# Two ConvLSTM recurrences: eighteen matmuls over 112 rows against fourteen over 128 packed rows per cell

## The reference, cut to what matters

```python
def step(carry, xr):
    h, c = carry
    inp = jnp.concatenate([xr, h], axis=1)          # 96 channels
    gates = lax.conv_general_dilated(inp, w_mid, (1,), 'SAME', dimension_numbers=dn) + b[None, :, None]
    i, f, g, o = jnp.split(gates, 4, axis=1)         # 4 x 48 channels, 3 taps along the width
    c2 = jax.nn.sigmoid(f) * c + jax.nn.sigmoid(i) * jnp.tanh(g)
    h2 = jax.nn.sigmoid(o) * jnp.tanh(c2)
    return ((h2, c2), h2)
_, hs = lax.scan(step, (z, z), x_rows, reverse=reverse)
```

## Time and profile before

| what | value |
|---|---|
| median of three runs | 2088.05 us (2082.49 to 2180.3) |
| the profiled execution's own time | 2081.32 us |
| its span, first to last instruction | 2079.5 us |
| around the span | 1.8 us |
| mean granted TensorE clock | 0.943 of full speed |
| first and last matmul of L668 | 278.1 and 1488.0 us |
| busy: TensorE, VectorE, ScalarE, GpSimd | 1838.4, 1388.5, 1064.7, 708.4 us |

### The profile page before, as it was taken

One profiled execution on the slowest core, in us unless ns is written; L12 is line 12 of the kernel. 1 busy time (PEld: TensorE's weight loads), 2 busy tenths in 40 slices (PEclk: granted clock), 3 DMA queues, 4 the chain that ended last, 5 costly groups with the idle time before them and its releaser, 6 DMA issues. The chain is left out here.

```text
span 2079.5 us, 43778 instructions
## 1 busy us (share of the span) xinstructions
PE 1838.4 (88%) x16306; PEld 1197.7 (58%) x16306; DVE 1388.5 (67%) x2550; ACT 1064.7 (51%) x1961; POOL 708.4 (34%) x583
## 2 busy tenths in 40 slices
PE   6979269999999999509999999999835999999999
PEld 5545147777777777207777777777512545555555
DVE  5538968888888888457888888888674234333434
ACT  1116147777777776346777777777561222222320
POOL 2010046666666655225666666665300000000000
PEclk9999679999999999759999999999976999999999
DMA  1769320000000000850000000000193001110100
GB/s 65 258 197 213 98 61 23 23 23 23 23 23 23 24 23 10 136 145 25 23 23 23 23 23 23 24 23 23 21 183 82 18 18 33 33 28 23 33 18 26
DMA packets 74618, 111.10 MB, mean 53 GB/s; under 512 B 11856, under 2 KB 31152, under 8 KB 74512
## 3 DMA queue, kind: packets, MB, share of 16 engines
q1 hardware_dynamic: 74512, 109.50, 20.3%
HBM read 71.71 MB, written 37.75 MB: 53 GB/s over the span
## 5 line engine op out<-in xcount | busy, mean ns | idle before, releaser
L668 PE MATMUL gates_l<-xh_l,w_hi_l 112*112 112x512 f32 x3072 | 819.5, 402 | 117.1 <-DVE keep_l L730 117.1
L668 PEld LDWEIGHTS gates_l<-xh_l,w_hi_l 112*112 112x112 f32 x3072 | 537.7, 175 | 315.4 <-issue 117.8
L644 POOL TENSOR_TENSOR xh_l<-xf_l,xh_l 48x512 fp32r<-48x512 f32 x256 | 360.1, 1407 | 281.8 <-ACT xh_l L687 281.4
L668 PE MATMUL gates_l<-xh_l,w_lo_l 112*112 112x512 f32 x1536 | 450.5, 402 | 0.0
L639 POOL TENSOR_TENSOR xh_l<-hs,xh_l 48x512 fp32r<-48x512 f32 x254 | 303.2, 1194 | 173.8 <-DVE hs L759 173.8
L668 PEld LDWEIGHTS gates_l<-xh_l,w_lo_l 112*112 112x112 f32 x1536 | 270.1, 176 | 97.9
L1174 PE MATMUL b_dw<-b_hid,b_diag 32*32 32x512 f32 x9120 | 313.1, 599 | 0.0
L699 ACT ACTIVATE gate_if_l<-gates_l 112x512 f32<-112x512 f32 x256 | 153.0, 598 | 246.9 <-PE gates_l L668 246.9
L739 DVE TENSOR_TENSOR keep_l<-gate_if_l,cell_l 48x512 f32<-48x512 f32 x256 | 175.5, 685 | 140.8 <-ACT gate_if_l L699 140.8
L1174 PEld LDWEIGHTS b_dw<-b_hid,b_diag 32*32 32x32 f32 x9120 | 185.7, 103 | 116.0 <-issue 48.3
L748 DVE TENSOR_TENSOR cell_l<-keep_l,add_l 48x256 f32<-48x256 f32 x512 | 196.7, 428 | 26.6
(11 more groups left out here) (148 smaller groups left out, 1236.4 us busy)
## 6 DMA issues: line engine op xcount, KB each, us to landing
xf_l<-rows SPq DMA_DIRECT2D x256, 96.0 KB, 2.0
hs<-rows SPq DMA_DIRECT2D x32, 384.0 KB, 10.3
rows<-hs SPq DMA_DIRECT2D x32, 384.0 KB, 5.0
xr<-in_x_rows SPq DMA_DIRECT2D x24, 256.0 KB, 2.7
xc<-in_x_cols SPq DMA_DIRECT2D x24, 256.0 KB, 3.0
mixed<-stage SPq DMA_DIRECT2D x24, 256.0 KB, 3.0
edged<-stage SPq DMA_DIRECT2D x24, 256.0 KB, 3.2
mixed_sb<-mixed SPq DMA_DIRECT2D x32, 192.0 KB, 3.7
```

The lines of the kernel that those rows point to most:

```text
L644: pool.tensor_tensor(xh[far[d]:far[d] + C, d, s, 1, :, 1:W + 1], xf[far[d]:far[d] + C, s, :].rearrange("p (b w) -> p b w", b=B), xh[far[d] ...
L668: mm = nc.tensor.matmul(ps[d][m][0:K, :], weight[:, d, m, t, :], xh[0:K, d, s, part, :, t:t + W], start=(first and t == 0), stop=(last and ...
```

## The change

- **The products are packed into 128 partitions.** The unused 16 + 16 rows of the operand (partitions 48 to 63 and 112 to 127) get channels 0 to 31 of the rounded x row, and the remaining 16 channels get a tile `xc` of their own, in which the three taps stand below each other (3 x 16 rows, twice, and two rows of ones for the bias). A cell step then has seven operands for each of the two banks: q = 0 on `xc`; q = 1 to 3, one for each tap, on a tile "HI" = [hi of h | lo of x | hi of x, channels 0 to 31]; q = 4 to 6 on a tile "LO" = [lo of h | hi of h again | the same x rows]. 2 x 7 = 14 matmuls. The weights lie in one tile `w` of 128 x 3136, staged through the unused part of `hs`; a `mask` says for which rows of q = 0 to 3 the rounded weight is subtracted from the whole one (which gives lo) and for which not.
- **DMAs bring the packed rows.** `spread(d, s)` on SyncE: four DMAs from one SBUF tile to another for each cell step, after TensorE is done with the tiles of that row. The x rows of both directions are loaded into one tile.
- **VectorE computes the state once, unrounded, in two halves into `hs` (L841). ScalarE rounds it from there into the HI tile, in two halves (L749, `state_hi`), and copies it once more into the LO tile (L756, `copy_state`)**, both while it works on the other direction's step: rounding between the sigmoid of i, f and the tanh of g, copy between that tanh and the sigmoid of o.
- **The rounding of the x rows goes to VectorE** (L819), one instruction for both directions, once per row instead of two.
- The tanh of g stays in PSUM and is multiplied there (L773, L830), and `cell` is one bank, added in one instruction (L834).

The diff, cut to its core:

```diff
--- before.py
+++ after.py
+        raw = hs[:, H // 2:H // 2 + WROWS, :].rearrange("p a n -> p (a n)")[:, 0:NW]
+        w = sb("w", [P, 2, NCH, 2, K], F32R)
...
-        xh = sb("xh", [P, 2, 2, 2, B, WP], F32R)
+        xs = sb("xs", [P, 2, FLAT + 2 * LEAD], F32R)
+        xh = sb("xh", [P, 2, 2, 2, FLAT], F32R)
+        xc = sb("xc", [P, 2, 2, FLAT], F32R)
...
+                def spread(d, s):
+
+                    for a in range(2):
+                        some = x_rows(s, slice(far[d] + a * GAP, far[d] + (a + 1) * GAP)).bitcast(F32)
+                        sp.dma_start(xh[a * HALF + C:(a + 1) * HALF, d, s, :, :].bitcast(F32), some.unsqueeze(1).broadcast_to([GAP, 2, FLAT])
+                                     ).then_inc(x_spread[d][s], 16)
+                    rest = xs[far[d] + 2 * GAP:far[d] + C, s, LEAD - 1:LEAD - 1 + FLAT].bitcast(F32)
+                    shifts = bass.AP(rest.tensor, rest.offset, [list(rest.ap[0]), [1, 3], [1, FLAT]])
+                    for c in range(2):
+                        sp.dma_start(xc[3 * GAP * c:3 * GAP * (c + 1), d, s, :].bitcast(F32), shifts).then_inc(x_spread[d][s], 16)
...
+                        if s < more:
+
+                            sp.wait_ge(x_lo[0], ahead)
+                            sp.wait_ge(x_lo[1], ahead)
+                            load(row_f, row_b, 1 - s)
+                        for d in range(2):
+                            sp.wait_ge(gates[d][1], done)
+                            if d == 0:
+                                sp.wait_ge(x_hi, split)
+                            spread(d, s)
...
+                    pool.wait_ge(x_hi, t + 1)
+                    if not (isinstance(t, int) and t < 2):
+                        pool.wait_ge(gates[d][1], t - 1)
+                    pool.tensor_tensor(inner(xh[f:f + C, d, s, HI, :]), wide(xf[f:f + C, s, :]),
+                                       inner(x_rows(s, slice(f, f + C))).bitcast(F32), ALU.subtract).then_inc(x_lo[d], 1)
...
+                            pe.wait_ge(x_spread[d][s], SPREAD * k + SPREAD)
+                            pe.wait_ge(sig_if[d], 2 * k + (s + 1))
+                            pe.wait_ge(sig_o[d], 2 * k + (s + 1))
+                            pe.wait_ge(cells[d], 2 * k + (s + 1))
+                            for m in range(2):
+                                chunk(m, 0, xc[:, d, s, :], 1, first=True)
+                            pe.wait_ge(x_lo[d], 2 * k + (s + 1))
+                            pe.wait_ge(h_hi[d], 2 * k + (s + 1))
+                            for m in range(2):
                                 for t in range(3):
-                                    mm = nc.tensor.matmul(ps[d][m][0:K, :], weight[:, d, m, t, :],
-                                                          xh[0:K, d, s, part, :, t:t + W],
-                                                          start=(first and t == 0), stop=(last and t == 2))
-                                return mm
+                                    chunk(m, 1 + t, xh[:, d, s, HI, :], t)
+                            pe.wait_ge(h_copy[d], 2 * k + (s + 1))
+                            pe.wait_ge(h_lo[d], 2 * k + (s + 1))
                             for m in range(2):
-                                taps(m, w_hi, 0, True, False)
-                                taps(m, w_lo, 0, False, False)
-                            pe.wait_ge(h_lo[d], 2 * k + s + 1)
-                            for m in range(2):
-                                taps(m, w_hi, 1, False, True).then_inc(gates[d][m], 1)
+                                for t in range(3):
+                                    mm = chunk(m, 4 + t, xh[:, d, s, LO, :], t, last=(t == 2))
+                                mm.then_inc(gates[d][m], 1)
...
+                def state_hi(t, row, d, s):
+
+                    n = near[d]
+                    for j, part in enumerate(parts):
+                        act.wait_ge(h_full[d], t * 2 + (j + 1))
+                        hi = nc.scalar.activation(padded(xh[n:n + C, d, s, HI, :])[:, j * HB:(j + 1) * HB, 1:W + 1],
+                                                  state(row, d)[:, part].rearrange("p (b w) -> p b w", b=HB), ACT.Copy)
+                    hi.then_inc(h_hi[d], 1)
+
+                def copy_state(row, d, s):
+
+                    f = far[d]
+                    nc.scalar.activation(inner(xh[f:f + C, d, s, LO, :]), wide(state(row, d)), ACT.Copy).then_inc(h_copy[d], 1)
...
+                            act.wait_ge(gates[d][0], 2 * k + (s + 1))
                             nc.scalar.activation(gate_if[0:K, d, :], ps[d][0][0:K, :], ACT.Sigmoid).then_inc(sig_if[d], 1)
...
+                            if some:
+                                state_hi(earlier, row, 1 - d, slot)
+                            act.wait_ge(gates[d][1], 2 * k + (s + 1))
+                            nc.scalar.activation(ps[d][1][n:n + C, :], ps[d][1][n:n + C, :], ACT.Tanh).then_inc(tanh_g[d], 1)
+                            if some:
+                                copy_state(row, 1 - d, slot)
+                            nc.scalar.activation(gate_o[f:f + C, d, :], ps[d][1][f:f + C, :], ACT.Sigmoid).then_inc(sig_o[d], 1)
+                            act.wait_ge(cells[d], 2 * k + (s + 2))
                             for j, part in enumerate(parts):
-                                act.wait_ge(cells[d], 4 * k + 2 * s + (j + 3))
...
+                                nc.scalar.activation(tanh_c[f:f + C, j, 0:PART], cell[f:f + C, part],
                                                      ACT.Tanh).then_inc(tanhs[d], 1)
...
+                    nc.vector.tensor_copy(w[:, d].rearrange("p a b c -> p (a b c)"), raw[:, d * per_d:(d + 1) * per_d]
+                                          ).then_inc(w_hi, 1)
...
+                    dve.wait_ge(w_hi, d + 1)
+                    for q, chunks in enumerate((slice(0, 1), slice(1, 4))):
+                        part = w[:, d, chunks].rearrange("p a b c -> p (a b c)")
+                        whole = raw[:, d * per_d + chunks.start * 2 * K:d * per_d + chunks.stop * 2 * K]
+                        nc.vector.scalar_tensor_tensor(part, part.bitcast(F32), mask[:, d, q:q + 1], whole, ALU.mult, ALU.add
+                                                       ).then_inc(w_ready, 1)
...
+                def split_hi(t, r):
+
+                    dve.wait_ge(x_in[r], 16 * t - 16 * r + 32)
+                    if not (isinstance(t, int) and t < 2):
+
+                        for d in range(2):
+                            dve.wait_ge(x_spread[d][r], (t - r) * (SPREAD // 2))
+                            dve.wait_ge(x_lo[d], t - 1)
+                    nc.vector.tensor_copy(inner(x_rows(r, slice(0, K))), wide(xf[0:K, r, :])).then_inc(x_hi, 1)
...
+                            dve.wait_ge(sig_if[d], 2 * k + (s + 2))
+                            dve.wait_ge(cells[d], 2 * k + (s + 1))
+                            nc.vector.tensor_tensor(keep[n:n + C, :], gate_if[f:f + C, d, :], cell[f:f + C, :],
+                                                    ALU.mult).then_inc(kept[d], 1)
+                            dve.wait_ge(tanh_g[d], 2 * k + (s + 1))
+                            nc.vector.tensor_tensor(ps[d][1][n:n + C, :], gate_if[n:n + C, d, :], ps[d][1][n:n + C, :],
                                                     ALU.mult).then_inc(added[d], 1)
...
+                            dve.wait_ge(kept[d], 2 * k + (s + 1))
+                            dve.wait_ge(added[d], 2 * k + (s + 1))
+                            nc.vector.tensor_tensor(cell[f:f + C, :], keep[n:n + C, :], ps[d][1][n:n + C, :], ALU.add
+                                                    ).then_inc(cells[d], 1)
+                            dve.wait_ge(sig_o[d], 2 * k + (s + 2))
                             row = 2 * k + s if d == 0 else k * -2 + (H - 1 - s)
                             whole = hs[n:n + C, bass.ds(row, 1), :].rearrange("p a n -> p (a n)")
+                            for j, part in enumerate(parts):
+                                dve.wait_ge(tanhs[d], 4 * k + (2 * s + j + 1))
+                                nc.vector.tensor_tensor(whole[:, part], gate_o[f:f + C, d, part], tanh_c[f:f + C, j, 0:PART],
+                                                        ALU.mult).then_inc(h_full[d], 1)
+                        if s < more:
+                            split_hi(2 * k + (s + 3), 1 - s)
+                for r in range(3):
+                    split_hi(r, r % 2)
+                with dve.Fori(0, H // 2 - 2) as k:
                     step(k)
+                step(H // 2 - 2, more=1)
+                step(H // 2 - 1, more=0)
```

244 lines of the change are left out of this document (122 added, 122 removed).

## The result

| what | before | after |
|---|---|---|
| median | 2082.82 us, 5 runs | 2065.48 us (2062.27 to 2067.98), 5 runs |
| profiled span | 2079.5 us | 2063.5 us |

The ratio is 0.9914, 95% interval 0.9893 to 0.9935: 0.9% faster, where 1.3 to 1.7% slower was predicted. The time lies in the range and inside 2%, but the sign is wrong: against the profiled execution the forecast was +34 us and the measurement is -16. Of the kernel before, one of the five runs took 2180.3 us; the ratio is of the fast runs and leaves it out.

A forecast was written before the change was run, and what follows sets the result against it. The prediction took TensorE to bound the kernel before and the ScalarE-VectorE loop after. Two layers, each 10.2 us more in cell steps and 7 at the start, added 34.4 to 2081.3: 2116 us, range 2055 to 2175.

The forecast's parts named there:

- The loop through ScalarE and VectorE: Cell step: tanh g, product, sum, tanh of the cell, sigmoid and roundings set the pace, 4.35 us from tanh g to tanh g.
- the sum of the loop: Cell step: durations, hand-overs and 0.02 us gaps added to 4.35 us, taken as 4.38, 10.2 us slower for each layer.
- a sign of being wrong: Cell step in the profile after: a step under 4.3 or over 4.45 us would show the forecast wrong.
- The start: Start of each layer: first matmul 17.8 us after the barrier, first sigmoid 22.5; with hold-up and end, 7 us more a layer.
- Rival 1: Cell step: roundings are cheap and TensorE's way binds, step 4.18 us, total 2065 us; chance 0.15.
- Rival 2: Cell step: ScalarE's wait for the cell vanishes and its busy time binds, 3.99 us, total 2017 us; chance 0.07.
- Rival 3: Cell step: the way through the state binds via 0.26 us hand-overs at register-held addresses, 4.71 us, total 2199 us; chance 0.30.
- Rival 4: VectorE's cast collides with GpSimd, waiting up to 1.41 us, `keep` 1.1 us late once a row, total 2252 us; chance 0.05.
- Rival 5: SyncE or the packed rows' landing binds; at 1.0 us per DMA a cell step takes 5.0 us, total 2273 us; chance 0.05.

The follow-up runs named there:

- sequence B: Four 48x256 ScalarE activations added ahead of the changed kernel's first step, destination partitions 0 and 64 in turns: starts 0.43 and 0.42 us apart; whole run 2062.09 us.
- sequence E: Same added run (2062.09 us), four activations with sources SBUF partition 0 and PSUM partition 64 in turns: first start 0.42 us behind, then 0.29 and 0.31.
- The run on the start: Kernel with the cast between `keep` and product, plus another order ahead of the loop (x rounding first, row 2's load earlier, GpSimd clearing `xc`): 2028.27 us, ratio 0.9737.
- F: Four 48x256 ScalarE activations added ahead of the changed kernel's first step, sigmoid and tanh in turns, equal partitions: starts 0.28 and 0.26 us apart; whole run 2062.09 us.

## Why the prediction was wrong

**What bounds the kernel after it: right.** The loop through ScalarE and VectorE was named, with ScalarE waiting for the sum alone (104.7 us in 256 waits, 0.3 to 0.44 each; predicted 0.3), the copy and sigmoid o for nothing, TensorE idle with slack of 0.2 to 0.3 on its way, SyncE and DMA hidden. All of it stood up to the experiments that took a part away.

**The step that failed is the sum of the loop, 4.35 us, taken as 4.38: it adds up single durations as if no activation could start before the one ahead has ended.** The step came out at 4.11, under the 4.3 that the prediction had named as a sign of being wrong. Measured from start to start on the two intervals of the timeline above, term for term:

| from, to | predicted | 401.69 to 405.62 | 405.62 to 409.92 |
|---|---|---|---|
| tanh g to product | 0.61 | 0.60 | 0.76 |
| product to sum | 0.80 | 0.81 | 0.79 |
| sum to tanh of the cell | 0.73 | 0.73 | 0.73 |
| tanh of the cell to sigmoid | 0.71 | 0.54 | 0.65 |
| sigmoid to rounding | 0.62 | 0.62 | 0.62 |
| rounding to tanh g | 0.88 | 0.63 | 0.75 |
| sum | 4.35 | 3.93 | 4.30 |

VectorE's terms and hand-overs hit within 0.01, but for the cast's 0.15. The durations of single activations hit too: L749 at 407 ns (0.42), L773 at 569 (0.56), L779 at 342 a piece. What missed is that I laid them end to end with a gap of 0.02 each. Two pieces that follow each other with equal partitions overlap by 0.07 to 0.09 us, about 0.1 against durations with a gap, and four such seams lie in the loop for the one direction, two for the other. The mean gain of these rows is 0.31. One term went the other way: the cast, which I had priced at nothing on the critical path (half a cast in VectorE's busy time only), holds `keep` and so the product back by 0.15 every second step, 0.08 in the mean. 4.35 - 0.31 + 0.08 = 4.12, against 4.11 measured. At 127 intervals and two layers the error is 0.27 x 254 = 69 us, and it turns +10 a layer into -24.

The recurrences of before show next to no such seam: L701 and L702 change partitions and start 0.62 apart for 0.59, and L708's pair waits for the sum's halves, 0.69 for two of 0.349. But the last stage of the same trace shows it:

```profile
1605.19 1.26 ACT L1242 ACTIVATE b_h<-b_dw,b_bias_r 128x512 f32<-128x512 f32 x2 [8.82 <-PE b_dw L1174]
1606.34 1.27 ACT L1236 ACTIVATE b_hid<-b_ex,b_bias_h 128x512 f32<-128x512 f32 x2
```

These work on all 128 partitions, so the start partition stays. A single L1242 takes 0.68 us and a single L1236 0.69, two of them take 1.26 and 1.27, and L1236 starts 0.11 us before L1242's pair has ended. So this trace spoke against a plain sum of durations, outside the stage that is changed. The Trainium skill, page "ScalarE: Activation LUTs", section "What ACT_TABLE_LOAD costs", says that back-to-back activations overlap by about 93 ns; the traces agree where partitions stay (0.07 to 0.09 us in the loop, 0.11 in the rows above), and not where they change (sequence B: starts 0.43 apart for durations of 0.42). Its page "VectorE: DVE Perf Modes", section "Two Vector instructions with no wait between them", has the condition, on the start quadrant of the last access to the same memory, for VectorE; sequence E shows it on ScalarE, for partitions 0 and 64.

**The start: right in kind, too small.** Predicted 7 us a layer, measured 13. The first matmul came 19.8 us after the barrier and not 17.8: SyncE took 2.9 us to issue the first four DMAs of packed rows (I had 1.4; two take 1.40 and 1.53, where I took 0.48 a piece from small loads). The first sigmoid came 4.7 us after that, as predicted. VectorE's hold-up by row 2's load was 4.8 us and not 1.6, again the 16 DMAs, 10.7 us in the queue instead of 7.7. The run on the start bought 19 us back.

**Rivals.** Rival 1 gave 2065 us, the time that came out, and is false: with two matmuls less nothing changes. It hits by luck, through errors that cancel: a step of 4.18 (4.11 measured) against 7 us for the start (13) and nothing for the 5 us outside the recurrences. Rival 2, the vanishing wait, did not come by itself; the halved sum brings it about. Rival 3 needed hand-overs of 0.26 that are 0.12 to 0.16. Rival 4 is real in mechanism: the cast and GpSimd lengthen each other when they meet, 0.66 for 0.43 and 1.30 for 1.20, but as the schedule said they do not meet in the changed kernel, and the price is a fraction of the 1.1 us I gave it. The cast of 112x512 never waited out a whole GpSimd instruction in the steps; in the start of the reordered kernel one took 1.04. Rival 5: the DMA share came out at 0.68, twice my 0.35, though the bytes were near those I reckoned, 104 GB/s against 23 + 80; the half of it that was taken away had cost nothing all the same.

**The 5 us outside the recurrences** are of the size by which single executions differ. The stretch between the recurrences and the one behind them take 92.2 and 587.4 us before, together 679.6, and 95.4 and 589.4 after, together 684.8. In the twelve experiments, none of which touches these stages, they take 88.9 to 94.0 and 585.6 to 592.6, together 677.3 to 684.4. No run shows that the change costs anything there.

## What to carry to other kernels

Price a chain on ScalarE from start to start, not by durations: where the start partitions of source and destination stay those of the last access to the same memory, each seam gives back about 0.1 us, which decided the sign here. Look for it in every stage of the trace, not only in the one that is changed. When an engine's busy share says that it has slack, ask where in its order the slack lies: a 0.43 us cast placed at the wrong one of three idle stretches cost 18 us. And when a time matches a rival's number, test its mechanism before believing it.

## What the runs showed of the hardware that was not expected

- ScalarE's overlap and its condition, above: 0.30 to 0.33 us from start to start for copies of 256 columns with equal partitions, 0.42 to 0.43 with a changed one; from PSUM 0.26 to 0.28 against 0.39. A change between sigmoid and tanh costs nothing (0.26 to 0.28 in F).
- A hand-over to a ScalarE instruction with a register-held address took 0.12 to 0.16 us, to a VectorE one 0.15 to 0.25 (404.17 to 404.42 and 408.24 to 408.39), to a GpSimd one 0.26 before and 0.19 to 0.21 after.
- A DMA from one SBUF tile to another with a three-dimensional pattern takes SyncE 0.58 to 0.75 us to issue (median 0.60) and lands after 2.4 to 3.0 us, where the loads of `xf` take 0.33 in the median and land after 2.1.
- Traffic of 104 GB/s at a DMA share of 0.68 left the compute instructions as long as they were: `keep` takes 685 ns before and after, and 686 at a share of 0.30.
